# A two-layer decoder on one core: the fp8 FFN two groups behind the front instead of three, four X buffers instead of five, and a new order of work

## The reference

```python
x = _layernorm(x + _L0_attn_ref(x, ...))    # causal attention, one head of 256
x = _layernorm(x + _L0_xattn_ref(x, k, ...)) # products of x and ctx, causal convolution, sum over products with ctx
x = _layernorm(x + _L0_ffn_ref(x, ...))     # ternary weights, int8-like rounding, silu gate, 256 -> 1024 -> 256
x = _layernorm(x + _L1_attn_ref(x, ...))    # r, k, v; cumulative sum of k*v with decay; norm over sequence and width
x = _layernorm(x + _L1_xattn_ref(x, ctx, ...)) # 16 query heads, 4 key heads of 128, softmax over 128 context rows
x = _layernorm(x + _L1_ffn_ref(x, ...))     # fp8 products, gelu gate, 256 -> 1024 -> 256
```

## Time and profile before

| | |
|---|---|
| median of 3 runs | 990.24 us (990.1 to 2268.74) |
| the profiled execution | 989.49 us, span of its instructions 987.7 us |
| mean granted clock of TensorE | 0.949 of full speed |
| busy: PE, DVE, ACT, POOL | 88%, 74%, 50%, 26% of the span |
| instructions | 14447 |
| read from HBM, written | 25.64 MB, 2.10 MB |

### The profile page before, as it was taken

How to read it: one execution, slowest core, us unless ns; L and a number is a source line. 1 busy time by engine, 2 the same in 40 slices (tenths; PEclk the granted TensorE clock), 3 DMA queues, 4 the chain that set the end, 5 groups by cost and what they waited for, 6 DMA issues and landing times.

```text
span 987.7 us, 14447 instructions
## 1 busy us (share of the span) xinstructions
PE 870.5 (88%) x5066; PEld 688.7 (70%) x5066; DVE 726.7 (74%) x1735; ACT 490.4 (50%) x1249; POOL 260.3 (26%) x298
## 2 busy tenths in 40 slices
PE   5756669998989899998999999999999999999964
PEld 4534557786778667976788677876688768777742
DVE  2769857968696879787868777977877876754543
ACT  3354123555543575347542665328642575476742
POOL 0417113223152220513134211531134211310100
PEclk9868788999999999999999999999999999999985
DMA  7752100010001000010001000010000000000000
GB/s 258 247 185 96 22 11 1 12 22 1 22 1 23 0 12 22 1 22 1 22 12 22 1 12 11 11 22 1 23 1 1 1 12 1 1 2 11 11 11 11
DMA packets 37064, 28.67 MB, mean 29 GB/s; under 512 B 18688, under 2 KB 34560, under 8 KB 36608
## 3 DMA queue, kind: packets, MB, share of 16 engines
...
HBM read 25.64 MB, written 2.10 MB: 28 GB/s over the span
## 4 chain that ended last, share of the span: by engine, by line
PE 40%; DVE 35%; ACT 11%; issue 9%; POOL 2%; DMA 1%; SPq 1%; DVEq 0%; POOLq 0%; ACTq 0%
PE bank L941 6%; PE bank L1121 5%; PE bank L1211 4%; DVE S L870 4%; ACT S L567 3%; PE bank L1128 3%; PE bank L1200 3%; PE bank L1190 2%; DVE S L877 2%; PE bank L1114 2%; PE bank L1000 2%; DVE mx L873 2%; PE bank L1001 2%; DVE amax L759 2%; DVE X L633 2%
## 5 line engine op out<-in xcount | busy, mean ns | idle before, releaser
L567 ACT ACTIVATE S<-S,mx 128x128 f32<-128x128 f32 x256 | 99.4, 392 | 59.7 <-DVE mx L873 59.4
L1121 PE MATMUL bank<-XTE,w_xq 128*128 128x256 f32 x512 | 124.1, 386 | 2.9 <-ACT QA L541 1.9
L1211 PE MATMUL bank<-w_xo,OX 128*128 128x256 f32 x512 | 116.0, 380 | 0.0
L540 ACT ACTIVATE QS<-bank,per_partition_sb 128x256 f32<-128x256 f32 x128 | 60.4, 472 | 99.3 <-PE bank L1121 97.9
L1121 PEld LDWEIGHTS bank<-XTE,w_xq 128*128 128x128 f32 x512 | 94.6, 192 | 20.3 <-ACT QA L541 5.0
L1211 PEld LDWEIGHTS bank<-w_xo,OX 128*128 128x128 f32 x512 | 95.7, 190 | 14.7 <-issue 1.9
L870 DVE SCALAR_TENSOR_TENSOR S<-bank,rq,xmask 128x128 f32<-128x128 f32 x256 | 71.7, 342 | 17.5 <-PE bank L1190 14.9
L332 POOL TENSOR_TENSOR rq<-vq,minus_half 128x8 f32<-128x8 f32 x32 | 52.4, 1639 | 119.6 <-DVE vq L843 119.6
L231 POOL TENSOR_TENSOR prod<-XTA,ccolA 128x256 f32<-128x256 f32 x96 | 63.9, 695 | 47.0 <-PE bank L1001 34.4
L1190 PEld LDWEIGHTS bank<-KTX,QA 128*128 128x128 f32 x512 | 64.6, 194 | 13.2 <-issue 10.8
L1190 PE MATMUL bank<-KTX,QA 128*128 128x128 f32 x512 | 68.4, 279 | 2.2 <-ACT OX L576 2.2
...
## 6 DMA issues: line engine op xcount, KB each, us to landing
...
taps_sb<-in_taps SPq DMA_DIRECT2D x1, 2048.0 KB, 10.9
...
w_xq<-in_L_xattn_Wq SPq DMA_DIRECT2D x1, 2048.0 KB, 11.3
w_xo<-in_L_xattn_Wo SPq DMA_DIRECT2D x1, 2048.0 KB, 16.2
...
```

The costliest lines, as they stand in the source:

```text
L567: ins = nc.scalar.activation(S[:, b, seq(h)], S[:, b, seq(h)], ACT.Exp, bias=mx[:, b, h:h + 1], accum_out=sm[:, b, h:h + 1])
L1121: ins = nc.tensor.matmul(cols(EQ)[:, h], w_xq[:, k, hh * XDIM:(hh + 1) * XDIM], XTE[:, k], start=k == 0, stop=k == HALVES - 1)
L1211: ins = nc.tensor.matmul(rows(EY)[:, b], OX[:, h, b], w_xo[:, n * XGROUP + h], start=n == 0 and h == 0 and b == 0, stop=n == XKV - 1 and h ...
```

## The change

AHEAD goes from 4 to 3. By it the sequence in `station_a` becomes F0 F1 F2 N0 F3 N1 F4 N2 F5 N3 F6 N4 F7 N5 N6 N7, where it was F0 F1 F2 F3 N0 F4 N1 F5 N2 F6 N3 F7 N4 N5 N6 N7; there are four X buffers; and a front waits for the FFN three groups before. All five strings of ORDER are new. Nothing else changes, and every step consists of the same instructions.

```diff
-AHEAD = 4
+AHEAD = 3
 XBUF = AHEAD + 1
 ...
 ORDER = {
     "pe": (
-        "sassaasaaaasaaaaaaaasasaacaqcqaacacaacaaaacaaccacacccacacacaqqcqcaaqcaqacqxaqyacqxaqyxaqycaqyxaccq"
 ...
+        "sassaasaaaasaaaaaasaaasqcqacaacaaccaacccacaaacacccacacacaqqqcaqcqacqaxycqqcxyqyaxqaocyqccqcaxqaqcyac"
 ...
```

More of the change, by code:

```diff
@@ L1225 @@
     "pe": (
[L1226 to L1230, removed]
@@ L1231 @@
-        "qxqoqcayxqyaaccqcayxaqxocaqccacaqcacaaqacayqyaxaxyqxaqoqxyqxyqxyqcocxyqxycqxocqyqcqxayqxyaqcyqccxqco"
-        "qcyqccqcyqcxycxqxacqyayoqxyqxaqxoqaaxqayxyqxaqyoqxaqyxaqyaqyxqaoqyxaqyxqyxaaqaaoxqyxyxyaoaxyayxaoaaa"
-        "aaaaaaaaaaa"
+        "sassaasaaaasaaaaaasaaasqcqacaacaaccaacccacaaacacccacacacaqqqcaqcqacqaxycqqcxyqyaxqaocyqccqcaxqaqcyac"
+        "cycaycqcxaaacyxqyxaaqaqxaoqyxqxqoycqycxqxcqocqxqycqaxqaxqacxqaccyacyqaaqaacqyxcaxyqaayccaqaocqaayxca"
+        "aaoaayxcaayaxyaxqoqyxqxyqoqcqacqaqxcayqacqxacyqxaaqaaqyqyxoqacqaaccxqcyaqyaxycxqcyaaycaxaxcaacqacaqa"
@@ L1234 @@
+        "caoaqxyqoxqxyqyqcoqcxyqacqayqacxqaycayqxaxaaqacoqccqcaqyayaqycxaqacycyaxacxaacqaaacxqaaxacoaqyxqoyqy"
+        "xqcxqcocxqcyxaqacxqyaqyaqacoyxaaccaacqqcqacxyayxayxcacqacqoqaxaycqyxayxacaayxayxqaaqaqoaqoqqcqcaqxac"
+        "qaycaqaxcqyaaqaaxqxyqyoqacqaaccqyxacqayxqcyacaacaacaacqaacaqcaxyoyqxyqxqxocqyxcqyxqcxqcyqoxcqxyqycxq"
+        "yoccqcaxqxcyaxccqcqycaqcyxaqxcqyaqyoqaaxqyaaqoxqxqyqyxqyoqxqyxaqyaqyqxaoyqyxaqyqxaqxyoyqaayxaaxxoyxy"
+        "xoaaaaaaaaa"
     ),
     "dve": (
-        "aasasasassaaasaassaaaaaaaaaaaaaasasassaascassacaqaqcaqacacaaacacaacaacaacaaaacaaacacaaacacccacaccacc"
@@ L1237 @@
[L1237 to L1241, removed]
@@ L1242 @@
-        "xycxcqcccqcyccqxyacqxacqyaxaaxqyqaqxayxaoyoaaqxyaxyaqaayxaaxyaqxyxyaaaoaoaaaaaaaaaaaaaa"
+        "aasasasassaaaasasasaaaaaaaaasaasasasasasasccaqaqaqcaacacacccccaacaacacaaaaaaacccacaacacaacacaccaaaqq"
+        "cqcxycxayacccccaqacycxycaxqaaacccaacycacyaaacaacxaaaxaqaaqaacqycqyxxcqqcoqxcoxyccaccacqyacxacaacaaxa"
+        "aqyaycaaaccaacqaayaxaacyaaxacaaaacaacaaaayxqaxyaqcqcooqqcaqxacxyacyaaaaaqcacaxacacxcqyacyaccayxaqyxc"
+        "aacaaaacaaacaqacacaaqaacaqacaxayxcycqqoqcoyxycaxacacacaaqccaacayaxaqcyacxcaayqyacacaacxacaaxaaqaacaa"
@@ L1243 @@
+        "aqcaqaaaaaccayxaycxcqqcoxcqxocyayccacacacaacaacaqacxayaxycaaccqaxyaxcyaacqcaayxayaxacaaaacaqaaaaqaaq"
+        "aaccoqoqcqaxcaxyacyaaaaacaqcacacacxqyxacyacacaqyaycaaacaaacaacaaqaaacaacaqacxqcxayaccxyxqqcqcxyxcyoc"
+        "ccccqoxycxcycaccqcxcaxcycaqycqcaqaaqxyaaxyaqqqxyxoyoaqyxayxaqyayxaaqxyaayxaxooaaaaaaaaa"
     ),
     "act": (
-        "sssaaasasassssscaacascascacsccccccccaaaacqqcqcacccxqycqxcqxyqyccxqyqcxyccqyqxyxycqxyqxcycqaxacxyccax"
-        "ycqacqyqxqacyqyxcxyqxcccqyxqayaxcayxaycqyaaxcxaaqyxcqccxyxycaxacqqcxyaqaxyqcaqycyqccxqqyxcyaxyaxacqy"
@@ L1247 @@
-        "acxaaxqcaxaccqxycycxyyqxaaqcqacqaxycyxcqyaqycxqqyxcaaxcyqaxcayqxaayxycxaacqycxcycxyxqqxyqxyqaacacaqy"
-        "qcycxacqqyxcxayqaxyxqcayxcyacxcqaacyxaacxycyqqyqxqcxyyaacaqaxyqxcaccqqyyxxyxqxycqxyqxcycxyxyccxcqqyc"
-        "qxcyaqxyacqcyqxcyqccqyxxyaxyayqxqxaaqxyaxayxyxqyqxaqyxaqyaqxayqxyaaxyqaayxqxyxyaxyaxyayxaaaaaaaaaaaa"
+        "sssaaasasassssscscsacasacacccaccccccqcqqccaacccxqyqacyxqcayxqccqayqxcyccyqyxyxqxxycxqyqycxqycxxcccxq"
+        "cqaxyqacxqacacyaaqaaxqcyxycyqaaacaqxyayxyxyxyxcxyqxyqqcacacaxqcacyqxaaqaaxqycycqxqcaacyaqxayqyxcyxcy"
@@ L1250 @@
+        "acxxyqxqyxcqxyyccqaycqxacqacyxqaycaacxaaqcqcyxqyaayaqcxaycycaxxxyxqyqxcyqyxcxccxccxaqyacxqcayqyaqaac"
+        "aacqcxyqcxyaayxacaqxyqaxyyxyxyxqxyqcqccaacxaqccayqaaqaaxqcxycyqqcaxayacqaxyqyxcayccyxyqxqcxyqxcyxcyx"
+        "ccqcxqyxcqxcyqyccxyqxaqxcyaccqyxaqxayyaaxqaayqxyqxxyyqxyqxqyaxqyaqyaxyqyxaqyxaqyaxyaaxyxxyxyxaaaaaaa"
         "a"
@@ L1252 @@
     "pool": (
-        "sasaaaaaaaacsqaqaacacaacaacccacaaqcaaacqcaqaccqcqcqqccaaaqoaaacqcaccqcqqacaqcoaaqacacaaqccaqcqqcaqac"
-        "coaqacaaqaaccqacqqcqcaaoqcaacaaqcaacqaqcqcqcaaoqcaaaqcacaacqqaqcqcocqcqcqccqqqaoqqaqoaa"
+        "sasaaaaaaacsaqqcaaaccaaacccacaqccaqaacqcacaacqacqqqcocqcaaqcaaqaacaacaqcqoqcaqcaqcaaqcaaaacqcqacqocc"
+        "qaaqcqacaaaaacqqcacqoccacqacqaaacqaaacqqacoqcaqcaqcaaqacaaacqcqacqcocqccqcqcqqaqoqqqaoa"
     ),
     "sp": (
-        "asasqsasassasaaqaqaaoqaaoqaaoqaaqoqoooo"
+        "asasqsassassaaqaaqoaaqoaaqoaaqoaaqoqooo"
     ),
```

## The result

The change takes **1004.55 us** (median of 20 runs, 995.56 to 1007.94); the kernel before takes 991.56 us beside it (20 runs, 19 of them between 989.9 and 994.3, one far off at 2268.74). The ratio of the means, without that one, is 1.0113, with a 95% interval of [1.0091, 1.0135]: slower by 1.1% (by the medians 1.3%), where the prediction said 989 and no change. The profiled execution of the change took 998.07 us, one of its quicker ones. It is 8.6 us longer in span than that of before (996.3 against 987.7), so its rows show some two thirds of what the medians show (13 us).

A forecast was written before the change was run, and what follows sets the result against it. PE's work order was taken as nearly the bound from 145 us on, group 0's middle through DVE before it; -7.5 + 0 + 9 - 1.9 = -0.4 against 989.49 gave 989 us, with 8 of 10 in 972 to 1010.

The forecast's parts named there:

- The start: Up to group 0's cross attention: starts 13.5 us earlier, less 5.9 of delayed PE work; net -7.5, bounds 0 and -15.
- Group 0's cross attention: From its start to its last output: less PE and DVE work there, counted 0, between -5 and +5 us.
- The middle: Behind group 0's output: close pairs, scores and gate products wait 12 us more, 9 taken; bounds 0 and 20.
- The last cross attention: Last round, with its filler gone: 3.6 us of waits walked against 0.5 before, +3.
- The tail: Behind the last output: group 7's FFN earlier, -9.7; group 6's FFN work moved ahead, +3.5; eighth gelu load, +1.3.
- The sum: Whole kernel: -7.5 + 0 + 9 - 1.9 = -0.4 us against 989.49, said as 989.
- (1): Rival: start -15, cross attention -5, middle 0, tail -6, nothing given back; 964 us; chance 0.11 with what lies beyond 970.
- (2): Rival: the chain through the X buffers binds, +20, close pairs +3; 1012 us; chance 0.14 with what lies beyond 1009.
- (3): Rival: last cross attention held by its own trips, tail term +5 instead of -1.9; 996 us, inside the forecast's 0.75.

The follow-up runs named there:

- e1: The change with five X buffers instead of four, AHEAD still 3 and the orders unaltered; 1004.2 us, ratio 1.014 to the kernel before.
- e2: The change with each squares product (L1128) streaming 64 columns of ones instead of one; 983.13 us, ratio 0.9931 to the kernel before.
- e5: The change with 15 PE steps of other programs brought forward between query steps and the next step on their bank; 1016.09 us, ratio 1.0217.
- e6: The order of e5 with the squares (L1128) streaming 64 columns of ones instead of one; 1005.43 us, ratio 1.0142 to the kernel before.
- e9: The kernel before (AHEAD 4) with the change's order up to the last squares of group 0's cross attention; 989.43 us, ratio 0.9975.
- e12: e2 with the end of group 6's FFN put back behind group 7's last output product; 995.59 us, ratio 1.0047 to the kernel before.

## Why the prediction was wrong, step by step

- **The start, -7.5: right.** L1053 came at 64.29 (62 to 65 forecast) and the cross attention's transposition at 129.22, 16.3 us earlier where "13.5 earlier" was forecast; the first L1121 behind it came at 131.0, inside 130 to 136. Net of PE work -10.2. In the nine profiled executions with the new start (the change, e1, e2, e5, e6 and e9 to e12) that transposition began between 129.22 and 132.10, 7.5 to 10 us earlier net, so what lies beyond the forecast is the spread of executions.

```profile
64.29 0.62 PE L1053 MATMUL bank<-ident_bf,QQ 128*128 128x128 bf16 x8 [0.38 <-DVE QQ L744]
...
```
```profile
129.22 1.09 PE L935 MATMUL bank<-ident,X 128*128 128x128 f32 x4 [4.45 <-DVE X L633]
```

- **Group 0's cross attention, 0:** -1.7, within its bounds. "The output of group 0 ending near 260" was wrong: it ended at 245.4, as 15 us less PE work stood ahead of it. It didn't follow from the prediction's own terms either: 132 and a stretch of 127 us with 10 us less work in it make 249.
- **The middle, +9: the step that failed.** Its waits were fewer than counted: idle time rose by 4.4 us against the 9 of the term, while the one pair with nothing between waited 1.66 where 1.65 was used. Idle time from there to the last output was 40.0 us, inside the 35 to 45 named. What was missing is a term for the clock. The sum took every step at the duration of before, since the middle's granted clock stood at 0.99 in the earlier trace rows; in the change it was 0.96 to 905, and that cost 17.3 us in this stretch. The text named this ("a granted clock under 0.95 in the middle would make everything longer") but put no price and no chance on it, and took the wrong line: 0.96 was enough. With it the middle came to 21.7, above the value of 9 and the upper bound of 20; without it, it would have been half the value.
- **The last cross attention, +3:** +3.2 against before. e12 (with wide squares) has such waits without the FFN steps too, so they belong to the round in the new order and were not brought by these steps.
- **The tail:** -4.7 where -9.7, +3.5 and +1.3 make -4.9. The tail behind the last L1211 is 31.5 us long, under the 33 named. The eighth gelu load is there and lies on the path. L935 of group 7 starts 0.15 us behind the end of its L633.

```profile
967.68 0.73 DVE L633 TENSOR_SCALAR X<-UE,mv_e,rstd_e 128x256 f32<-128x256 f32 x2 [0.81 <-POOL rstd_e L332]
...
968.56 1.08 PE L935 MATMUL bank<-ident,X 128*128 128x128 f32 x4 [3.80 <-DVE X L633]
...
981.68 1.28 ACT L491 ACT_TABLE_LOAD   x1
982.97 2.00 ACT L491 ACTIVATE G<-G 128x1024 bf16<-128x1024 bf16 x2
```
```profile
L491 ACT ACT_TABLE_LOAD  x8: 1283/1283/1283, 270.1 to 981.7; - x8
```

The gelu starts 0.01 us behind its load, so here again there is no drain to see on top of it.

- **The sum.** -10.2 -1.7 +21.7 +3.2 -4.7 = +8.3, within 0.3 of the 8.6 that the spans show (rounding and missing records). Start, group 0's cross attention and the middle's waits together came out 9.0 us better than counted (2.7, 1.7 and 4.6), which by luck hid half of the 17.3. Without the 17.3 it would be -9. The medians show 13 because the profiled execution had more clock than most: the five shortest executions of the change have a mean clock of 0.928 to 0.936, the four near 1008 have 0.920 to 0.922.
- **The rivals.** (1) wanted -20 up to the last output of group 0 and 0 in the middle; measured were -11.9 and +21.7. (2) gave a time near the measured one (1012) by waits of some 20 us, which the change's idle time doesn't have: luck. (3), with its tail of +5, is answered by e12.

What stays open: why 7 more waits near a squares step go with 8 more low stretches, when 10 of the 14 in the kernel before have none. That the new order's low clock comes from these pairs is argued from their places; what is shown is that the low clock goes when the squares are widened. The half-microsecond waits of the change come two and three together around one squares step, which fits, but no run varied that alone, and e5 took waits ahead of squares away without the clock coming back. Why the wait of 3.22 us went either way is open too.

The Trainium skill, "TensorE: Matmul & The Clock Gate", A second HAM failure mode: psum-queue depth-cycling, tells of a kernel in which PE idled for moments between groups of products, often enough that the clock went back and forth between its two levels. The trace of the change agrees: the waits at the low stretch that begins at 357.1 are 0.52, 0.52 and 0.53 us.
